# Segment mean with 16-bit operands: three-part edge features and one-hots built tile by tile

## The reference, cut to what matters

```
def _L0_gnn_ref(x, edge_index, edge_attr):
    dst = edge_index[1]
    sums = segment_sum(edge_attr, dst, num_segments=3125)
    counts = segment_sum(ones(100000), dst, num_segments=3125)
    denom = where(counts > 0, counts, 1)
    return sums / denom[:, None]

x = _layernorm(x + _L0_gnn_ref(x, edge_index, edge_attr_16))
x = _layernorm(x + _L1_gnn_ref(...))   # two message passes, edge_attr_48
x = _layernorm(x + _L2_gnn_ref(...))   # edge network, edge_attr_2
x = _layernorm(x + _L3_gnn_ref(...))   # two graph convolutions
```

## Time and profile before

| | |
|---|---|
| median of three runs | 4370.68 us |
| the profiled execution | 4369.29 us, its span 4367.5 us |
| granted clock over the span | 0.906 |
| PE busy | 3568.2 us (82%) |
| DVE busy | 3444.2 us (79%) |
| POOL busy | 2951.8 us (68%) |
| ACT busy | 2056.7 us (47%) |
| PE matmuls of the segment mean (L512, `vals`) | 258.8 us, 1168 |
| PE matmuls of the same line in the edge network (`v`) | 1168 more |

### The profile page before, as it was taken

The page is one execution under the profiler, slowest core; times in us unless marked ns, Lnnn a source line. Parts: engine busy times, 40 slices in busy tenths (PEclk is TensorE's granted clock), DMA queues, the critical chain, the costliest instruction groups (busy, mean ns, idle before and its releaser), DMA issues.

```text
span 4367.5 us, 92806 instructions
## 1 busy us (share of the span) xinstructions
PE 3568.2 (82%) x27877; PEld 3016.5 (69%) x27878; DVE 3444.2 (79%) x6087; ACT 2056.7 (47%) x2171; POOL 2951.8 (68%) x2849
## 2 busy tenths in 40 slices
PE   3997999999999699999999957777766666666665
PEld 3995888888888477777777757777755555555554
DVE  7667999999999688888888878888756777566676
ACT  0106999999999599999999900000000000000000
POOL 1325777777777477777777657766437777477776
PEclk9999999999999799999999977777668888688887
DMA  4002111111111321111111111111011111111111
GB/s 51 26 19 24 24 24 24 24 24 24 24 24 23 23 29 31 30 31 30 31 30 31 23 29 30 28 27 25 13 22 34 33 33 33 23 34 33 33 33 24
DMA packets 260307, 121.63 MB, mean 28 GB/s; under 512 B 165614, under 2 KB 222450, under 8 KB 260278
## 3 DMA queue, kind: packets, MB, share of 16 engines
q1 hardware_dynamic: 172470, 90.58, 8.5%
q0 software_dynamic: 87808, 30.68, 7.0%
HBM read 119.25 MB, written 1.78 MB: 28 GB/s over the span
## 4 chain that ended last, share of the span: by engine, by line
PE 31%; POOL 30%; issue 21%; DVE 11%; DVEq 2%; DMA 1%; ACT 1%; SPq 1%; POOLq 0%; ACTq 0%
POOL gb L384 15%; POOL gb L374 15%; PE ps L581 9%; PE ps L597 9%; PE ps L512 7%; PE ps L587 2%; DVE oht L1139 2%; DVE oh L881 1%; ACT v L490 1%; DVE xt L970 1%; PE ps L528 1%; DMA gb<-table,idx 1%; PE ps L703 1%; DVE gb L1174 1%; DVE v L1153 1%
## 5 line engine op out<-in xcount | busy, mean ns | idle before, releaser
L384 POOL DMA_INDIRECT gb<-table,idx x1568 | 1615.6, 1030 | 554.6 <-issue 418.1
L374 POOL DMA_INDIRECT gb<-table,idx x1176 | 1256.4, 1068 | 592.1 <-issue 354.0
L581 PE MATMUL ps<-big,oh 128*128 128x290 f32 (+1 forms) x7840 | 1263.5, 308 | 1.6 <-DVE big L1010 1.6
L581 PEld LDWEIGHTS ps<-big,oh 128*128 128x128 f32 x7840 | 1068.9, 190 | 124.7 <-DVE big L1010 2.2
L597 PE MATMUL ps<-w,ht 128*128 128x320 f32 x3136 | 1008.3, 444 | 95.5 <-DVE xt L970 93.9
L451 ACT ACTIVATE oh<-iota_f,src_n 128x640 fp32r<-128x640 f32 x1372 | 1024.7, 815 | 0.0
L454 ACT ACTIVATE oh<-oh,ones 128x2560 fp32r<-128x2560 f32 (+1 forms) x392 | 849.4, 2167 | 12.7
L597 PEld LDWEIGHTS ps<-w,ht 128*128 128x128 f32 x3136 | 557.3, 191 | 356.7 <-DVE xt L970 165.4
L970 DVE TENSOR_TENSOR xt<-ps,gb 128x640 f32<-128x640 f32 x784 | 642.5, 820 | 90.7 <-PE ps L597 25.6
L703 PE MATMUL ps<-tabb,oht 128*128 128x240 bf16 x3920 | 527.7, 294 | 110.2 <-DVE mk L1209 98.2
L978 DVE TENSOR_REDUCE msg<-xt 128x80 f32<-128x1280 f32 (+1 forms) x392 | 580.4, 1481 | 0.0
(11 more groups left out here) (212 smaller groups left out, 2576.5 us busy)
## 6 DMA issues: line engine op xcount, KB each, us to landing
gb<-table,idx POOLq DMA_INDIRECT x2744, 2.3
eat<-in_eat SPq DMA_DIRECT2D x196, 192.0 KB, 2.4
eat<-vtab SPq DMA_DIRECT2D x147, 256.0 KB
ea<-in_edge_attr SPq DMA_DIRECT2D x98, 64.0 KB, 1.8
idx<-in_dst SPq DMA_DIRECT2D x196, 4.0 KB, 1.5
idx<-in_src SPq DMA_DIRECT2D x147, 4.0 KB, 1.5
ea<-in_edge_attr SPq DMA_DIRECT2D x1, 784.0 KB, 19.4
table<-tabb SPq DMA_DIRECT2D x2, 300.0 KB, 4.4
```

The source lines that it names most:

```text
L374: nc.gpsimd.indirect_dma_start(out=gb[:, b, t, 0:tabw[p]], out_offset=None, in_=tabs[p], in_offset=bass.IndirectOffsetOnAxis(ap=idx[:, b, ...
L384: nc.gpsimd.indirect_dma_start(out=gb[:, b, t, 0:tabw[p]], out_offset=None, in_=tabs[p], in_offset=bass.IndirectOffsetOnAxis(ap=idx[:, b, ...
L581: mm = nc.tensor.matmul(out, oh5[:, b, t, c * P:(c + 1) * P], big[:, b, t, 0:W], start=False, stop=False, skip_group_check=True)
```

## The change

- The features are split in three bfloat16 parts, not in two fp32r parts. `vals` becomes bfloat16 with 50 columns per tile (16 high, a one, 16 middle, 16 low, one unused), and PE's moving operand has 49 of them.
- The slots are now for a pair, and there are two: `vals[k]`, `ea16[k]`, k = pair mod 2. One ACTIVATE or one subtraction handles the 2 x 8 x 16 values per partition of a whole pair.
- ACT writes the high part (`high_part`), POOL subtracts it in place (`rest_of`), ACT writes the middle part (`mid_part`), DVE subtracts to the low part (`low_part`) and counts up `ea_lo`.
- `row_used[0]` begins at 2 and goes up by 1 per pair; the high part of pair p waits for p + 1.
- The one-hots (`oh_m`, bfloat16, in memory that was not used) are built by 8 TENSOR_SCALARs of 128x128 per supertile and block: the float16 row `iota_h` against one column of `dst_f` as a per-partition scalar. 16-bit floats hold the numbers exactly as both sides are shifted by 1600 (`MID`).
- Setup gets `iota_h` (one TENSOR_SCALAR of 3200 columns) and the shift of `dst_f`; behind the mean come one more addition (the third part) and the shift back.

The diff, cut to its core:

```diff
-        ea16 = sb("ea16", [P, 2, T, D])
-        vals = sb("vals", [P, 4, T, 2 * (D + 1)], F32R)
+        ea16 = sb("ea16", [P, 2, 2, T, D])
+        vals = sb("vals", [P, 2, 2, T, 3 * D + 2], BF16)
...
-            with sp.Fori(0, PAIRS) as i:
+            def load_pair(i, k):
+                sp.wait_ge(ea_lo, i * 2 + k + 1)
                 for b in range(2):
-                    sp.wait_ge(ea_lo, i * 2 + b + 1)
...
+            def rest_of(j, k):
+                pool.wait_ge(ea_hi, j + 1)
+                nc.gpsimd.tensor_tensor(ea16[:, k, :, :, :], ea16[:, k, :, :, :], vals[:, k, :, :, 0:D],
+                                        ALU.subtract).then_inc(ea_rest, 1)
...
+            def high_part(i, k):
+                act.wait_ge(ea_in[k], (i + 1) * 32)
+                act.wait_ge(row_used[0], i * 2 + k + 1)
+                nc.scalar.activation(vals[:, k, :, :, 0:D], ea16[:, k, :, :, :], ACT.Copy).then_inc(ea_hi, 1)
+            def mid_part(j, k):
+                act.wait_ge(ea_rest, j + 1)
+                nc.scalar.activation(vals[:, k, :, :, D + 1:2 * D + 1], ea16[:, k, :, :, :], ACT.Copy).then_inc(ea_mid, 1)
+            high_part(0, 0)
+            with act.Fori(0, QUADS) as i:
+                for k in range(2):
+                    high_part(i + k, 1 - k)
+                    mid_part(i * 2 + k, k)
+            mid_part(PAIRS - 1, 0)
...
-            pe.sem_inc(row_used[0], 4)
+            pe.sem_inc(row_used[0], 2)
...
-                pe.wait_ge(ea_cp, j * 2 + 2)
-                pe.wait_ge(ea_lo, j * 2 + 4)
+                pe.wait_ge(ea_lo, j + 3)
+                pair_windows(0, j, oh_m, lambda b, t: vals[:, k, b, t, 0:3 * D + 1], lambda c: psf[:, bass.ds(c * 64, 3 * D + 1)])
                 nc.tensor.matmul(ps[:, 6, 0:32], zeros[:, 0:P], zeros[:, 0:32], start=True, stop=True)\
-                    .then_inc(row_used[0], 2)
+                    .then_inc(row_used[0], 1)
...
+            link(V.tensor_scalar(iota_h[:, :], iota_f[:, :], -float(MID), None, ALU.add))
...
+            def low_part(j, k):
+                dve.wait_ge(ea_mid, j + 1)
+                V.tensor_tensor(vals[:, k, :, :, 2 * D + 1:3 * D + 1], ea16[:, k, :, :, :], vals[:, k, :, :, D + 1:2 * D + 1],
+                                ALU.subtract).then_inc(ea_lo, 1)
+            def mean_onehots(j):
+                lo, hi, off = load_window(dve, j, win2)
+                with dve.Fori(lo, hi) as c:
+                    for h in range(2):
+                        dve.wait_ge(oh_used[0][h], off + c + 1)
+                        for t in range(T):
+                            one = V.tensor_scalar(oh_m[:, h, t, :], iota_h[:, bass.ds(c * P, P)], dst_f[:, bass.ds(j * 2 + h, 1), t],
+                                                  None, ALU.is_equal)
+                        one.then_inc(oh_ready[0][h], 1)
+            low_part(0, 0)
+            with dve.Fori(0, QUADS) as i:
+                for k in range(2):
+                    mean_onehots(i * 2 + k)
+                    low_part(i * 2 + (k + 1), 1 - k)
+            mean_onehots(PAIRS - 1)
...
+            link(V.tensor_tensor(t1[:, :, 0:D], t1[:, :, 0:D], a0[:, :, 2 * D + 1:3 * D + 1], ALU.add))
```

More of the change, by code:

```diff
@@ L38 @@
 EH = 64
+MID = NP_ // 2
 MP = [2 * (MF + 1), 2 * D]
@@ L73, in build @@
             .rearrange("p b (t n) -> p b t n", t=T)
-        sb("rest", [P, 2 * T * (NH * MP[0] + CW) - NC * SUP - T * GW])
+        rest = sb("rest", [P, 2 * T * (NH * MP[0] + CW) - NC * SUP - T * GW])
+        iota_h = rest[:, 0:NP_ // 2].bitcast(F16)
+        oh_m = rest[:, NP_ // 2:NP_ // 2 + SUP].bitcast(BF16).rearrange("p (b t n) -> p b t n", b=2, t=T)
         dst_i = sb("dst_i", [P, NSUP, T], I32)
@@ L206, in build @@
         ea_in = [sem(f"ea_in{b}") for b in range(2)]
-        ea_cp = sem("ea_cp")
+        ea_hi = sem("ea_hi")
+        ea_rest = sem("ea_rest")
+        ea_mid = sem("ea_mid")
         ea_lo = sem("ea_lo")
@@ L289, in _ @@
             sp.dma_start(vtab, row_v).then_inc(s_vtab, 16)
-            with sp.Fori(0, PAIRS) as i:
+            def load_pair(i, k):
+                sp.wait_ge(ea_lo, i * 2 + k + 1)
                 for b in range(2):
-                    sp.wait_ge(ea_lo, i * 2 + b + 1)
-                    sp.dma_start(ea16[:, b, :, :].rearrange("p t f -> p (t f)"),
-                                 e16[bass.ds(i * 2 + b, 1), :, :].rearrange("o p f -> p (o f)")).then_inc(ea_in[b], 16)
+                    sp.dma_start(ea16[:, k, b, :, :].rearrange("p t f -> p (t f)"),
+                                 e16[bass.ds(i * 4 + 2 * k + b, 1), :, :].rearrange("o p f -> p (o f)")).then_inc(ea_in[k], 16)
+            with sp.Fori(0, QUADS) as i:
+                for k in range(2):
+                    load_pair(i, k)
+            load_pair(QUADS, 0)
             def store_table(p):
@@ L356, in _ @@
             pool.sem_inc(ea_lo, 2)
[L358 to L361, removed]
+            def rest_of(j, k):
+                pool.wait_ge(ea_hi, j + 1)
+                nc.gpsimd.tensor_tensor(ea16[:, k, :, :, :], ea16[:, k, :, :, :], vals[:, k, :, :, 0:D],
+                                        ALU.subtract).then_inc(ea_rest, 1)
             with pool.Fori(0, QUADS) as i:
[L364 to L367, removed]
+                for k in range(2):
+                    rest_of(i * 2 + k, k)
+            rest_of(PAIRS - 1, 0)
             def gather(p, b, seen):
@@ L501, in zero_bank, with pair_windows @@
                 return nc.tensor.matmul(ps[:, bk, :], zeros[:, 0:P], zeros[:, :], start=True, stop=False, skip_group_check=True)
-            def pair_windows(w, j, rhs_of, out_of):
+            def pair_windows(w, j, ohs, rhs_of, out_of):
                 lo, hi, off = load_window(pe, j, win2)
@@ L511, in pair_windows @@
                         for t in range(T):
-                            mm = nc.tensor.matmul(out, oh_r[:, h, t, :], rhs_of(h, t),
+                            mm = nc.tensor.matmul(out, ohs[:, h, t, :], rhs_of(h, t),
                                                   start=False, stop=False, skip_group_check=True)
@@ L551, in mean_step @@
             def mean_step(j, k):
-                pe.wait_ge(ea_cp, j * 2 + 2)
-                pe.wait_ge(ea_lo, j * 2 + 4)
-                pair_windows(0, j, lambda b, t: vals[:, 2 * k + b, t, :], lambda c: psf[:, bass.ds(c * 64, 2 * (D + 1))])
+                pe.wait_ge(ea_lo, j + 3)
+                pair_windows(0, j, oh_m, lambda b, t: vals[:, k, b, t, 0:3 * D + 1], lambda c: psf[:, bass.ds(c * 64, 3 * D + 1)])
                 nc.tensor.matmul(ps[:, 6, 0:32], zeros[:, 0:P], zeros[:, 0:32], start=True, stop=True)\
-                    .then_inc(row_used[0], 2)
+                    .then_inc(row_used[0], 1)
             with pe.Fori(0, QUADS) as i:
@@ L659, in edge_step @@
                 pe.wait_ge(vl_done, j * 2 + 4)
-                pair_windows(1, j, lambda b, t: v96[:, b, t, :, :].rearrange("p k f -> p (k f)"),
+                pair_windows(1, j, oh_r, lambda b, t: v96[:, b, t, :, :].rearrange("p k f -> p (k f)"),
                              lambda c: psf[:, bass.ds(pe.snap(c * EW + ((c * 52) >> 8) * (512 - EBANK * EW),
@@ L777, in _ @@
             link(V.memset(ones[:, :], 1.0))
-            link(V.memset(vals[:, :, :, D:D + 1].bitcast(F32), 1.0))
-            link(V.memset(vals[:, :, :, 2 * D + 1:2 * D + 2].bitcast(F32), 0.0))
+            link(V.memset(vals[:, :, :, :, D:D + 1], 1.0))
             link(V.memset(parts[0][:, :, :, MF:MF + 1].bitcast(F32), 1.0))
@@ L799, in _ @@
             V.tensor_reduce(ext[:, 1, :], neg_dst[:, :, :], AX.X, ALU.max).then_inc(s_ext, 1)
+            link(V.tensor_scalar(dst_f[:, :, :], dst_f[:, :, :], -float(MID), None, ALU.add))
             dve.wait_ge(s_extp, 1)
@@ L882, in pair_onehots @@
                                         ALU.is_equal).then_inc(oh_ready[w][h], 1)
-            with dve.Fori(0, PAIRS) as i:
-                pair_onehots(0, i)
+            def low_part(j, k):
[5 more added lines that the diff above has]
+                with dve.Fori(lo, hi) as c:
+                    c = nc.s_assert_within(c, 0, NB - 1, skip_runtime_bounds_check_because="a block index out of the window table")
+                    for h in range(2):
[6 more added lines that the diff above has]
+            with dve.Fori(0, QUADS) as i:
+                for k in range(2):
+                    mean_onehots(i * 2 + k)
+                    low_part(i * 2 + (k + 1), 1 - k)
+            mean_onehots(PAIRS - 1)
             def layer_norm(xx):
@@ L952, in _ @@
             dve.sem_inc(s_node, 1)
+            link(V.tensor_scalar(dst_f[:, :, :], dst_f[:, :, :], float(MID), None, ALU.add))
             for l in range(2):
```

## The result

The changed kernel takes 4452.15 us (median of 4 runs, 4444.45 to 4454.08), the kernel before 4369.35 (4 runs beside them, 4367.48 to 4373.97). The ratio is 1.0185, 95% interval 1.0167 to 1.0202: slower, 1 us from the 4451 predicted. The profiled execution has a span of 4449.6 us and a granted clock of 0.908 over it.

A forecast was written before the change was run, and what follows sets the result against it. PE bounded the segment mean; changed, a serial DVE-PE-ACT ring would. 49 turns of 5.78 us, less 0.86, plus 24 second blocks of 2.73 give 347.9, +81.1; with 4369.3 and +0.6 that is 4451 us, range 4412 to 4500.

The forecast's parts named there:

- ring: Segment mean: DVE, PE and ACT wait for each other in a circle, so a one-block pair costs the sum, 5.78 us.
- Low part to first one-hot: DVE's start of a pair in the segment mean, with window load and branch: 1.45 us.
- One-hots: Sixteen 128x128 one-hots on DVE in the segment mean, starts 0.161 us apart: 2.66 us.
- Last one-hot to ACT: Segment mean, DVE through PE's eight matmuls and then the small matmul to ACT: 0.85 us.
- High and middle part: ACT's two instructions in the segment mean: 0.74 us, then 0.08 to the next engine.
- Second block: Segment mean, a pair's second block adds sixteen one-hots and loop work: 2.73 us, for 24 pairs.
- Behind the mean: After the segment mean, the third addition is linked into the chain: 0.6 us; the shift back costs 0.
- Later stages: 0: Stages after the segment mean run the same instructions as before, so they add 0.
- B: Rival: one-hots in the segment mean don't overlap, starts 0.246 us apart; +99, 4550 us; chance 0.12.
- C: Rival: one-hots in the segment mean start 0.10 us apart; -70, 4381 us; chance 0.08.
- D: Rival: the ring isn't closed and DVE alone bounds the segment mean; stage 276 us, total 4379; chance 0.05.
- E: Rival, faster: D plus short one-hot spacing, PE and ACT hidden behind DVE; stage 205 us, total 4308; chance 0.03.

The follow-up runs named there:

- the open order: Changed kernel with ACT writing the middle part of pair j+1 before the high part of pair j+2: 4370.94 us, ratio 1.0003.
- the version at 4302 us: Changed kernel with middle part ahead of next high part, one TENSOR_TENSOR per half and window load ahead of the low part: 4302.05 us, ratio 0.9853.
- the kernel with the TENSOR_TENSOR: Changed kernel with one-hots built by one TENSOR_TENSOR per half from f32, written as bfloat16: 4407.61 us, ratio 1.0088.

## Why the prediction was right

Its sign, mechanism and size held: ring in place, 47 waits of DVE for ACT of 1.45 us, ACT's for the small matmul, neither POOL nor the loads ever a releaser in the turn. By its steps:

1. *Low part to first one-hot*, 1.45: measured 1.38 and, with the outer branch, 1.67, mean 1.52.
2. *One-hots*, 0.161 apart and 2.66 for sixteen: 0.249 long, (2.70 - 0.25)/15 = 0.163 apart, 2.70. The subtraction in the prediction is off: its 0.25 - 0.085 is 0.165, which would have given 2.73 for sixteen and about 5 us more for the stage, and lies as near to the measured spacing. The fixed part of the f32 form and the overlap seen at L1139 carried over to a width and form that the trace of before didn't have.
3. *Last one-hot to ACT*, 0.85: measured 0.65. The eight matmuls took 0.52, near the 0.50 assumed and not the 0.36 of the earlier trace rows. Whether a lower clock is why isn't shown, as the trace has no clock record there. But the small matmul starts 0.36 behind the first of the eight, inside their 0.52, and the term had it behind them.
4. *High and middle part*, 0.74 and 0.08: 0.75 and 0.03. A turn was 5.78 predicted; 5.51 and 5.80, mean 5.66, measured.
5. *Second block*, 2.73: measured 2.88. The one-hots of a two-block pair last 5.57 us and those of a one-block pair 2.69, both means over the stage.

The stage came to 345.1 for 347.9, the +81.1 to +78.3: terms 3 and 4 too dear by 0.24, 1 and 2 too cheap by 0.11, times 49, partly balanced by 24 x 0.15. Behind the mean +0.6 was right. *Later stages: 0* was not: they took 3.3 us more. So it is luck that the total came out to 1 us: it holds two misses of about 3 us that cancel.

Missed as well: PE's busy time, "under 60 us", is 77.9, as eight matmuls start 42 ns apart but each lasts 219; with PE idle for more than three quarters of the stage nothing depends on it. DVE's wait for ACT was put at 80 us and is 68.2, and the low part lasts 0.66 and not 0.42 because POOL's subtraction runs beside it. That was hidden here, as the window load ran beside it; with the window load placed ahead, the 0.66 is the whole step.

Of the rivals, B and C fall by the 0.163. D, with the ring open, was priced at 276 us for a stage that then measured 263.2 in the open order: DVE's window load hides better there than assumed, by enough to outweigh the 21 us by which POOL lengthens 47 of the one-hots. And E's condition, open ring and cheap one-hots at once, is what the version at 4302 us brings about.

## What to carry to other kernels

Before a queue is rewritten, walk once round it: if an instruction that waits for the consumer stands ahead of one that the producer needs, the engines' times can add up as here, and the bound is the sum, however idle each of them is. Here two ACT instructions in the other order were worth 82 us of 345, more than the cheaper one-hots with 33 or the earlier window load with 41. The order closes the ring only together with the two slots of `vals`; whether more slots would open it as well, no run here tried. And with the ring open, look at what runs beside the new bound: an idle engine's work can lengthen it.

## What the runs showed of the hardware

- DVE and POOL slow each other down where both work on SBUF: a DVE subtraction 0.42 alone and 0.66 beside POOL, the f32 one-hot 1.22 and up to 1.69, one 16-bit TENSOR_SCALAR of the open order up to 740 ns where the median is 242, POOL's subtraction 0.66 and up to 1.71. The Trainium skill (GPSIMD Engine Reference, "Specifications") says that the two share their SBUF interfaces, with contention beside DVE instructions that have two SBUF inputs or run in a two-port mode. The rows of DVE's instructions with two inputs agree; in which mode the TENSOR_SCALAR ran no row shows. That section gives no price.
- A 16-bit TENSOR_TENSOR with one repeated input ran no faster than with f32 inputs (1219 and 1220 ns).
- What stands ahead in DVE's program has a price: with 80 instructions that run once the ratio rose by 0.0029, some 13 us. What in the sequencer it is stays open. The row that moves in the first message layer is the wait for the sequencer ahead of `xt`, once a loop body: from 600 to 1300 us it comes to 13.3 us in 32 times in the kernel with the TENSOR_TENSOR, and to 17.1 in 32 times both with the 80 instructions and in the changed kernel. One such wait in the changed kernel and in the one with the TENSOR_TENSOR, 0.54 and 0.42:

```profile
704.68 0.82 DVE L1006 TENSOR_TENSOR xt<-ps,gb 128x640 f32<-128x640 f32 x1 [0.54 <-issue]
```

```profile
713.36 0.82 DVE L1002 TENSOR_TENSOR xt<-ps,gb 128x640 f32<-128x640 f32 x1 [0.42 <-issue]
```
